# Attention stages with small heads: row maxima lead the weighing by one group and three key tiles instead of two whole groups

## The chip, the cores and the metric

The kernel runs on one core of a Trainium2 chip. The metric is the device time of one execution in microseconds (us): 5284.45 as the median of three runs, 5282.03 to 5288.88. Engines: TensorE (PE; its weight loads are PEld), VectorE (DVE), ScalarE (ACT), GpSimd (POOL) and SyncE (SP), which here only issues DMAs.

## The reference, cut to what matters

The program is a decoder of four layers, each with a self-attention, a cross-attention and a feed-forward part, each followed by a residual and a layer norm. Five of its attentions are softmax attentions over 16 heads of 16 channels, on a batch of 4 with 512 queries, and use the routine that is changed. Their core is

```
scores = einsum('bhqd,bhkd->bhqk', q, k) * scale   (+ bias or mask, or causal)
attn = softmax(scores, axis=-1)
out = einsum('bhqk,bhkd->bhqd', attn, v)
```

The routine runs six times. In the order of the program, with the name that its tiles have in the trace:

| stage | tiles' name | keys | key tiles of 128 |
|---|---|---|---|
| coarse levels of the pyramid attention | pyr_coarse | 512 places, each query sees 256 or 128 of them | 4 |
| fine level of the same | pyr_core | 512 | 4 |
| context (cross-attention of layer 1) | l1x_core | 1024 | 8 |
| plain (layer 2) | l2a_core | 512 | 4 |
| causal with a linear bias (layer 3) | l3a_core | 512, lower triangle | 4 |
| masked (cross-attention of layer 3) | l3x_core | 1024, with a mask that is added | 8 |

A seventh attention (heads of 64 channels) has a routine of its own and is not touched.

## The kernel before

`attention_stage` (L256) treats a batch b in four groups g of four heads, so 16 groups in a row. A group needs two things. The first is the maximum of each row of scores: `pass_a` (L546) multiplies queries by keys in chunks of up to 512 keys (TensorE, L558) into PSUM banks A, and `maxima` (L715) reduces each chunk on VectorE (L734; with a mask L730, which adds the mask tile `mask_q` first). A group has 16 chunks with four key tiles and 32 with eight. In the causal stage the four chunks that stand beside tile t span (t+1) x 128 keys, while the score products of tile t span (4-t) x 128 queries. The maxima then travel as a row: `turn` (L565) transposes them on TensorE (L572), `negate` copies them out on VectorE (L748, L751), `split_max` cuts them into three bf16 parts on GpSimd (L813, L814, L816), and `row` on SyncE writes them with three DMAs of 4 KB (L473) into three rows of the group's query tile. At the start of each group TensorE waits for these rows (`row_in`), because the score product then subtracts the maximum by itself.

The second is the weighing: for key tile i, four score products (L626, one a head) into banks B, four exponentials on ScalarE (L693), and in the next tile `weigh`, the product of weights and values (L593). In the masked stage each bank B is first filled with the mask tile `mask_k`, three fills of four by ScalarE (L676) and one by VectorE (L758), three steps ahead of the score product that adds to it. ScalarE and VectorE run their lists in order: a fill that waits for `mask_k` holds back every exponential and every maximum behind it.

While group g is weighed, the maxima of group g+2 are taken, a fair share beside each tile. So before group 0 can start, the maxima of groups 0 and 1 are taken alone, and beside the last two groups there are none. `turn` for group g+1 comes after tile 0 of group g.

SyncE's list for group g (L511 to L534) sets when transfers start. It runs strictly in order:
- wait until group g-1 is weighed (that is the end of tile 0 of group g), then load the values of group g+1 (L445) and queries and keys of group g+3 (L442);
- the row of group g+1 (waits for `split_max`);
- g = 0: `gather_sums` of the batch before, two DMAs of 32 KB, one after the other (L486, L488); VectorE's `invert_dense` waits for them after tile 0 of group 1;
- g = 1: `return_inverses`, one DMA of 32 KB and then four of 256 KB (L495, L498); GpSimd multiplies by them in groups 2 and 3 (L837), two products a group, after `split_max`;
- g = 3: `make_dense` of the batch before, eight DMAs of 64 KB (L507), after GpSimd's last product;
- masked stage, g = 1: the four tiles of `mask_q` of the next batch, each as soon as the maxima of group 3 have used the old one (L449);
- masked stage, g = 3: the four loads of `mask_k` of the next batch, 512 KB for two key tiles each (L452).

The fine stage also finishes the last batch of the coarse stage, so there these steps occur once more.

Of the kernel before, what the change touches and what calls it, by code (L numbers as in the profile page):

```python
# [255 lines left out]
def attention_stage(k, name, q_store, k_store, values, nq, nk, scale, att, head_dim=HD, slopes=None, mask=None, spans=None, dense_att=None, carried=None,  # L256
# [42 lines left out]
    inverse_at = [(2 + p, 0) for p in range(4)]  # L299

    def chunks_of(i):

        some = list(range(i * NCH // nkt, (i + 1) * NCH // nkt))
        return [some[len(some) * j // heads:len(some) * (j + 1) // heads] for j in range(heads)]
# [9 lines left out]
    with ExitStack() as held:  # L314
# [66 lines left out]
        def later(b, g, ahead):  # L381

            return b + (g + ahead) // groups, (g + ahead) % groups

        def keys_of(qi, c):
# [51 lines left out]
        def _(sync):  # L437
# [73 lines left out]
            def group(b, g):  # L511
                before = later(b, g, -1)
                if exists(*before):
                    sync.wait_ge(pv_done, at(*before, nkt, nkt + ahead_tiles))
                    if exists(*later(b, g, 1)):
                        load_values(*later(b, g, 1))
                    if exists(*later(b, g, RING - 1)):
                        load_group(*later(b, g, RING - 1))
                if exists(*later(b, g, 1)):
                    row(*later(b, g, 1))  # L520
                if g == 0 and to_finish(b - 1):
                    gather_sums(b - 1)
                if g == 1 and to_finish(b - 1):
                    return_inverses(b - 1)
                if g == 3 and to_finish(b - 1):
                    make_dense(b - 1)
                if mask is not None and g == groups - 3 and exists(b + 1, 0):
                    for qi in range(nqt):
                        sync.wait_ge(a_taken, at(b, groups - 1, NCH + 1, (qi + 1) * NCH // nqt))
                        load_mask_q(b + 1, qi)  # L530
                if mask is not None and g == groups - 1 and exists(b + 1, 0):
                    for i in range(nkt // 2):
                        sync.wait_ge(exp_done, at(b, g, NS, 2 * (i + 1) * heads + 3))
                        load_mask_k(b + 1, i)  # L534
# [10 lines left out]
        def _(pe):  # L545
# [60 lines left out]
            turn(0, 0)  # L606
            pass_a(0, 1, range(NCH))

            def group(b, g):
# [3 lines left out]
                for i in range(nkt):  # L613
                    more = chunks_of(i) if exists(*later(b, g, 2)) else [()] * heads
                    qs, ks = queries_of(i), slice(i * P, (i + 1) * P)
                    for j in range(heads):
# [16 lines left out]
                        mm.then_inc(s_ready, 1)  # L633
                        pass_a(*later(b, g, 2), more[j])
                    if i:
                        weigh(b, g, i - 1)
                    elif exists(*later(b, g, -1)):
                        weigh(*later(b, g, -1), nkt - 1)
                    if i == 0 and exists(*later(b, g, 1)):
                        turn(*later(b, g, 1))  # L640
# [65 lines left out]
        def _(dve):  # L706
# [71 lines left out]
            negate(0, 0)  # L778
            maxima(0, 1, range(NCH))

            def group(b, g):
                before = later(b, g, -1)
                for i in range(nkt):
                    more = chunks_of(i) if exists(*later(b, g, 2)) else [()] * heads
                    for j in range(heads):
                        after = step_after(b, g, i * heads + j)
                        if after[2] in by_vector and exists(*after[:2]):
                            fill(*after, at(b, g, NS, i * heads + j + 3))
                        maxima(*later(b, g, 2), more[j])
                        if (i, j) in inverse_at and not small and exists(*before):  # L790
                            invert(*before, inverse_at.index((i, j)))
                    if i == 0 and exists(*later(b, g, 1)):
                        negate(*later(b, g, 1))
# [2053 lines left out]
```

## Time and profile before

| | us |
|---|---|
| median of the runs (three) | 5284.45 |
| the profiled execution, its own time | 5285.31 |
| its span, first to last instruction | 5283.5 |
| mean granted TensorE clock, share of full speed | 0.882 |

The profile is of one execution. "Busy" is the time in which an engine ran something; a line of a group of instructions names the source line, the engine, and output and input tiles. PEclk is the share of the full 2.4 GHz that TensorE was granted; 0.50 is 1.2 GHz. The stage of each row can be told by its tiles' name or its time: coarse 156 to 324, fine 338 to 547, context 1482 to 1899, plain 2250 to 2458, causal 4309 to 4484, masked 4638 to 5173 us.

### The profile page before, as it was taken

What the parts mean: (1) busy time and instruction counts of PE and PEld (TensorE: products, weight loads), DVE (VectorE), ACT (ScalarE), POOL (GpSimd) and SP (SyncE); (2) the same over time, 40 slices, a digit from 0 to 9 for tenths busy, and PEclk for the clock granted to TensorE, in tenths of its full rate; (3) what the DMA queues carried; (4) which work ended last, traced back from release to release, by engine and by line L of the source; (5) the groups of instructions that cost most, each with busy time, mean ns of one, the idle gap of its engine ahead of it and who ended that gap; (6) DMA issues with size and microseconds to landing.
All of it is one profiled execution on the core that took longest, in us unless ns stands there. A gap on an engine that the chain in (4) does not pass through costs nothing. (4 is left out here: it accounts for less than half of the span.)

```text
span 5283.5 us, 69474 instructions
## 1 busy us (share of the span) xinstructions
PE 4269.9 (81%) x20468; PEld 2003.2 (38%) x20468; DVE 2857.8 (54%) x6454; ACT 2371.7 (45%) x4625; POOL 1389.1 (26%) x1234
## 2 busy tenths in 40 slices
PE   7779665666789968497699799999997979669986
PEld 5323454664422238223344233333335634312223
DVE  4458374015678830386300367666763256578875
ACT  4447231232346744265333344444441236349993
POOL 3111151221300020312000177777772112200001
PEclk9679877787779979788799899999998989769998
DMA  8655202430543336544233311112111065733421
GB/s 297 145 107 121 62 1 57 154 119 13 199 120 79 91 126 231 163 98 110 98 153 153 116 64 57 57 57 68 59 41 43 1 186 121 250 103 106 105 66 37
DMA packets 461222, 559.20 MB, mean 106 GB/s; under 512 B 80804, under 2 KB 363924, under 8 KB 448452
## 3 DMA queue, kind: packets, MB, share of 16 engines
q1 hardware_dynamic: 453440, 520.11, 33.0%
q0 software_dynamic: 6384, 32.61, 1.9%
q8 instruction: 138, 2.26, 0.2%
q10 hardware_dynamic: 1068, 2.66, 0.2%
q14 instruction: 192, 1.57, 0.1%
HBM read 340.80 MB, written 200.54 MB: 102 GB/s over the span
## 5 line engine op out<-in xcount | busy, mean ns | idle before, releaser
L1190 POOL TENSOR_TENSOR lc_totals<-lc_totals,lc_weights 128x1024 f32<-128x1024 f32 (+1 forms) x320 | 615.6, 1924 | 187.5 <-DVE lc_totals L1139 158.8
L1099 ACT ACTIVATE lc_weights<-ps 128x1024 f32<-128x1024 f32 x384 | 393.1, 1024 | 560.7 <-PE ps L1019 560.5
L1120 DVE TENSOR_REDUCE lc_part_max<-ps 128x2 f32<-128x1024 f32 x384 | 466.4, 1215 | 316.0 <-PE ps L999 316.0
L1019 PE MATMUL ps<-lc_q,lc_k 64*128 64x512 f32 x1536 | 394.2, 591 | 0.0
L1029 PE MATMUL ps<-lc_weights,lc_v 128*64 128x512 f32 x1536 | 373.3, 606 | 0.9 <-ACT lc_sums L1086 0.7
L734 DVE TENSOR_REDUCE l1x_core_part_max<-ps 128x1 f32<-128x512 f32 x512 | 317.0, 683 | 84.5 <-PE ps L558 78.3
L730 DVE CUSTOM_DVE_ANT_0 l3x_core_unused<-ps,l3x_core_mask_q 128x512 f32<-128x512 f32 x512 | 330.6, 686 | 7.0 <-DVE l3x_core_row_max L738 4.9
L693 ACT ACTIVATE l3x_core_weights<-ps 128x512 f32<-128x512 f32 x512 | 326.1, 691 | 7.7 <-PE ps L626 7.4
L189 ACT ACTIVATE proj_value<-ps 128x512 f32<-128x512 f32 (+2 forms) x352 | 179.9, 519 | 320.2 <-PE ps L159 267.6
L693 ACT ACTIVATE l1x_core_weights<-ps 128x512 f32<-128x512 f32 x512 | 266.3, 603 | 89.0 <-PE ps L626 88.9
L676 ACT ACTIVATE ps<-l3x_core_mask_k 128x512 f32<-128x512 f32 x384 | 269.3, 701 | 28.9 <-DMA l3x_core_mask_k<-in_mask_k 28.9
L558 PE MATMUL ps<-l3x_core_k,l3x_core_q 96*128 96x512 bf16 x512 | 214.4, 420 | 52.7 <-DVE l3x_core_part_max L730 37.6
L1185 POOL TENSOR_TENSOR lc_totals<-lc_weights 128x1024 f32<-128x1024 f32 x32 | 75.4, 2356 | 615.9 <-ACT lc_weights L1099 604.8
L558 PE MATMUL ps<-l1x_core_k,l1x_core_q 96*128 96x512 bf16 x512 | 210.5, 414 | 23.1 <-DMA l1x_core_k<-k_parts 16.3
L218 POOL TENSOR_TENSOR proj_parts<-proj_rest,proj_parts 128x512 bf16<-128x512 f32 x112 | 136.8, 1224 | 338.5 <-ACT proj_parts L169 338.1
L1111 DVE MEMSET lc_ones_row<- 128x128 bf16 x1 | 0.2, 165 | 397.3 <-PEq L112 397.3
L626 PE MATMUL ps<-l3x_core_q,l3x_core_k 99*128 99x512 bf16 x512 | 198.1, 393 | 19.1 <-ACT ps L676 18.1
L1295 PE MATMUL ps<-ident,X 128*128 128x128 f32 x352 | 69.8, 340 | 163.4 <-DVE X L1332 156.4
L999 PE MATMUL ps<-lc_k_round,lc_q_round 64*128 64x512 bf16 x768 | 151.4, 390 | 59.8 <-DVE lc_part_max L1120 48.6
L626 PE MATMUL ps<-l1x_core_q,l1x_core_k 99*128 99x512 bf16 x512 | 193.0, 387 | 6.4 <-ACT l1x_core_weights L693 6.4
L1316 DVE SCALAR_TENSOR_TENSOR rn_z<-ps,rn_z 128x256 f32<-128x256 f32 x112 | 45.9, 418 | 261.6 <-PE ps L1287 235.4
L734 DVE TENSOR_REDUCE l2a_core_row_max<-ps 128x1 f32<-128x512 f32 x256 | 158.5, 681 | 47.2 <-PE ps L558 47.1
(467 smaller groups left out, 8787.7 us busy)
## 6 DMA issues: line engine op xcount, KB each, us to landing
cf_w<-in_L1f_w SPq DMA_DIRECT2D x32, 1024.0 KB, 7.8
values<-proj_value SPq DMA_DIRECT2D x112, 256.0 KB, 3.2
latent_k<-proj_value SPq DMA_DIRECT2D x96, 256.0 KB, 2.0
latent_values<-proj_value SPq DMA_DIRECT2D x96, 256.0 KB, 2.0
lc_k<-latent_k SPq DMA_DIRECT2D x32, 768.0 KB, 6.5
lc_v<-latent_values SPq DMA_DIRECT2D x32, 768.0 KB, 5.1
k_parts<-proj_parts SPq DMA_DIRECT2D x56, 384.0 KB, 2.6
q_parts<-proj_parts SPq DMA_DIRECT2D x40, 384.0 KB, 3.1
```

The costliest lines, as they stand in the source:

```text
L189: nc.scalar.activation(value[0:rows, j % VALUES, :, 0:d], k.ps[0:rows, n % 8, 0:H * d].rearrange("p (h d) -> p h d", h=H), ACT.Copy).then_ ...
L558: mm = nc.tensor.matmul(out, q_stack[r][0:rows_a, j, qs], k_stack[r][0:rows_a, j, keys], start=True, stop=not causal)
L626: mm = nc.tensor.matmul(out, k_stack[r][0:rows_b, j, ks], q_stack[r][0:rows_b, j, qs], start=not seeded, stop=not (causal or seeded), skip ...
L676: nc.scalar.activation(k.ps[:, B0 + (g * NS + s) % B_BANKS, 0:nq], seed, ACT.Copy).then_inc(filled, 1)
L693: nc.scalar.activation(weights[:, (g * NS + s) % WEIGHTS, qs], k.ps[:, B0 + (g * NS + s) % B_BANKS, qs], ACT.Exp, scale=scale).then_inc(ex ...
L730: nc.vector.tensor_tensor_reduce(unused[:, n % 2, :], scores, mask_q[:, qi, keys], 1.0, -3.0e38, ALU.add, ALU.max, out).then_inc(a_taken, 1)
L734: nc.vector.reduce_max(out, scores, AX).then_inc(a_taken, 1)
L1019: mm = nc.tensor.matmul(out[j], k_tile[g % RING][strip(j), i * P:(i + 1) * P], q_tile[g % RING][strip(j), :], start=False, stop=True)
L1029: mm = nc.tensor.matmul(k.ps[strip(j), ACC, 0:nq], v_tile[g % V_RING][:, i, strip(j)], weights[:, i % TILES, j, :], start=i == 0, stop=i = ...
L1099: nc.scalar.activation(weights[:, i % TILES, :, :], k.ps[:, B0 + (i % 2) * HEADS:B0 + (i % 2 + 1) * HEADS, 0:nq], ACT.Exp, scale=scale).th ...
L1120: nc.vector.reduce_max(own, k.ps[:, A0:A0 + HEADS, :], AX).then_inc(a_taken, 1)
L1190: nc.gpsimd.tensor_tensor(total, total, own, ALU.add).then_inc(added_by_pool, 1)
```

## The change

The maxima now lead by one group and three key tiles. Beside tile i of group g stand the chunks of tile i+3, of group g+1 as long as i+3 is within the group, of group g+2 after that. Before group 0, only the chunks of three tiles of group 1 are taken ahead (12 of 16, or 12 of 32). `turn` and `negate` for group g+1 move from tile 0 to tile 1 (four key tiles) or tile 5 (eight). The loads of `mask_q` move from group 1 to group 2 and ahead of the row. Everything else that follows the row in SyncE's list keeps its place behind it.

```diff
--- before.py
+++ after.py
@@ -297,6 +297,8 @@
     QUARTER = nq // 4
     SUMS = 2
     inverse_at = [(2 + p, 0) for p in range(4)]
+
+    FIRST_TILES = min(nkt - 1, 3)
 
     def chunks_of(i):
 
@@ -382,6 +384,15 @@
 
             return b + (g + ahead) // groups, (g + ahead) % groups
 
+        def chunks_beside(b, g, i):
+
+            tile = i + FIRST_TILES
+            found = later(b, g, 1 + tile // nkt)
+            return (*found, chunks_of(tile % nkt) if exists(*found) else [()] * heads)
+
+        first_chunks = range(FIRST_TILES * NCH // nkt)
+        turn_at = nkt - FIRST_TILES
+
         def keys_of(qi, c):
 
             if spans:
@@ -516,6 +527,10 @@
                         load_values(*later(b, g, 1))
                     if exists(*later(b, g, RING - 1)):
                         load_group(*later(b, g, RING - 1))
+                if mask is not None and g == groups - 2 and exists(b + 1, 0):
+                    for qi in range(nqt):
+                        sync.wait_ge(a_taken, at(b, groups - 1, NCH + 1, (qi + 1) * NCH // nqt))
+                        load_mask_q(b + 1, qi)
                 if exists(*later(b, g, 1)):
                     row(*later(b, g, 1))
                 if g == 0 and to_finish(b - 1):
@@ -524,10 +539,6 @@
                     return_inverses(b - 1)
                 if g == 3 and to_finish(b - 1):
                     make_dense(b - 1)
-                if mask is not None and g == groups - 3 and exists(b + 1, 0):
-                    for qi in range(nqt):
-                        sync.wait_ge(a_taken, at(b, groups - 1, NCH + 1, (qi + 1) * NCH // nqt))
-                        load_mask_q(b + 1, qi)
                 if mask is not None and g == groups - 1 and exists(b + 1, 0):
                     for i in range(nkt // 2):
                         sync.wait_ge(exp_done, at(b, g, NS, 2 * (i + 1) * heads + 3))
@@ -604,14 +615,14 @@
                     nc.tensor.matmul(k.ps[:, B0 + n, 0:nq], *operands, start=True, stop=False, skip_group_check=True).then_inc(opened, 1)
             pass_a(0, 0, range(NCH))
             turn(0, 0)
-            pass_a(0, 1, range(NCH))
+            pass_a(0, 1, first_chunks)
 
             def group(b, g):
                 r = g % RING
                 if small:
                     pe.wait_ge(row_in, 48 * at(b, g, 1, 1))
                 for i in range(nkt):
-                    more = chunks_of(i) if exists(*later(b, g, 2)) else [()] * heads
+                    beside_b, beside_g, more = chunks_beside(b, g, i)
                     qs, ks = queries_of(i), slice(i * P, (i + 1) * P)
                     for j in range(heads):
                         s = i * heads + j
@@ -631,12 +642,12 @@
                         if causal:
                             mm = nc.tensor.matmul(out[:, 0:P], k.ident_bf[:, :], k.above_k[:, :], start=False, stop=True)
                         mm.then_inc(s_ready, 1)
-                        pass_a(*later(b, g, 2), more[j])
+                        pass_a(beside_b, beside_g, more[j])
                     if i:
                         weigh(b, g, i - 1)
                     elif exists(*later(b, g, -1)):
                         weigh(*later(b, g, -1), nkt - 1)
-                    if i == 0 and exists(*later(b, g, 1)):
+                    if i == turn_at and exists(*later(b, g, 1)):
                         turn(*later(b, g, 1))
                     if i == spread_at and not small and exists(*later(b, g, -1)):
                         spread(*later(b, g, -1), at(b, g, 1, 2 if exists(*later(b, g, 1)) else 1))
@@ -776,20 +787,20 @@
                         fill(0, 0, s, 1)
             maxima(0, 0, range(NCH))
             negate(0, 0)
-            maxima(0, 1, range(NCH))
+            maxima(0, 1, first_chunks)
 
             def group(b, g):
                 before = later(b, g, -1)
                 for i in range(nkt):
-                    more = chunks_of(i) if exists(*later(b, g, 2)) else [()] * heads
+                    beside_b, beside_g, more = chunks_beside(b, g, i)
                     for j in range(heads):
                         after = step_after(b, g, i * heads + j)
                         if after[2] in by_vector and exists(*after[:2]):
                             fill(*after, at(b, g, NS, i * heads + j + 3))
-                        maxima(*later(b, g, 2), more[j])
+                        maxima(beside_b, beside_g, more[j])
                         if (i, j) in inverse_at and not small and exists(*before):
                             invert(*before, inverse_at.index((i, j)))
-                    if i == 0 and exists(*later(b, g, 1)):
+                    if i == turn_at and exists(*later(b, g, 1)):
                         negate(*later(b, g, 1))
                     if i == 0 and g == 1 and to_finish(b - 1):
                         invert_dense(b - 1)
```

## Rows read from the trace of the kernel before

**Rows 1.** The page's first part: busy us, share of the span, instructions.
```profile
PE 4269.9 (81%) x20468; PEld 2003.2 (38%) x20468; DVE 2857.8 (54%) x6454; ACT 2371.7 (45%) x4625; POOL 1389.1 (26%) x1234
```
**Rows 2.** Busy time by stretch: start:end, length, engines, PEclk, DMA share, GB/s; context stage.
```profile
1503.00:1520.90 17.90, 17.82 (x31) 3.14 (x30) 17.90 (x31) 0.00 (x0) 1.21 (x3) 0.50 0.00 1
```
**Rows 3.** The same view, masked stage: second pass of maxima, then groups 0 to 13.
```profile
4677.60:4701.30 23.70, 18.38 (x32) 3.24 (x31) 20.99 (x92) 0.00 (x0) 1.22 (x3) 0.50 0.00 1
4701.30:5113.90 412.60, 382.52 (x1800) 99.82 (x1798) 367.24 (x1502) 401.21 (x797) 26.96 (x50) 0.98 0.36 94
```
**Rows 4.** Timeline (start, duration, engine, line), context stage, two tiles without maxima.
```profile
1864.50 1.07 PE L593 MATMUL ps<-l1x_core_weights,l1x_core_v 128*32 128x512 f32 x8
1866.95 0.64 PE L593 MATMUL ps<-l1x_core_weights,l1x_core_v 128*32 128x512 f32 x4
```
**Rows 5.** Timeline, coarse stage before group 0: one chain of the row, queues empty.
```profile
161.46 0.38 PE L572 MATMUL ps<-ident,pyr_coarse_row_max 128*16 128x128 f32 x1 [0.44 <-DVEq L740]
163.76 1.86 SPq L473 DMA_DIRECT2D pyr_coarse_q<-pyr_coarse_max_parts  x3
166.85 0.39 PE L626 MATMUL ps<-pyr_coarse_q,pyr_coarse_k 99*128 99x256 bf16 x1 [0.37 <-DMA pyr_coarse_q<-pyr_coarse_max_parts]
```
**Rows 6.** Timeline of TensorE, fine stage: one group, from first score to first score.
```profile
396.28 0.39 PE L626 MATMUL ps<-pyr_core_q,pyr_core_k 99*128 99x512 bf16 x1
...
399.30 0.28 PE L572 MATMUL ps<-ident,pyr_core_row_max 128*16 128x128 f32 x1
...
407.95 0.39 PE L626 MATMUL ps<-pyr_core_q,pyr_core_k 99*128 99x512 bf16 x1
```
**Rows 7.** SyncE's queue in that group; DMA issues (count, KB, median us to landing).
```profile
399.43 0.39 SPq L445 DMA_DIRECT2D pyr_core_v<-values  x1
...
pyr_core_q<-pyr_core_max_parts SPq DMA_DIRECT2D x42, 4.0 KB, 3.7
```
**Rows 8.** Timeline of TensorE, causal stage: starts of tiles 0, 2, 3, next group.
```profile
4363.47 0.39 PE L626 MATMUL ps<-l3a_core_q,l3a_core_k 102*128 102x512 bf16 x1
...
4368.96 0.28 PE L626 MATMUL ps<-l3a_core_q,l3a_core_k 102*128 102x256 bf16 x1
...
4371.42 0.23 PE L626 MATMUL ps<-l3a_core_q,l3a_core_k 102*128 102x128 bf16 x1
...
4373.73 0.39 PE L626 MATMUL ps<-l3a_core_q,l3a_core_k 102*128 102x512 bf16 x1
```
**Rows 9.** Coarse stage: TensorE's tiles 0 and 1; and who TensorE waited for.
```profile
201.96 0.39 PE L626 MATMUL ps<-pyr_coarse_q,pyr_coarse_k 99*128 99x256 bf16 x1 [1.05 <-DMA pyr_coarse_q<-pyr_coarse_max_parts]
...
204.36 0.38 PE L572 MATMUL ps<-ident,pyr_coarse_row_max 128*16 128x128 f32 x1
...
207.40 0.29 PE L626 MATMUL ps<-pyr_coarse_q,pyr_coarse_k 99*128 99x128 bf16 x1
...
PE ps L626 <- DMA pyr_coarse_q<-pyr_coarse_max_parts: 33.5, 14, 5.5
```
**Rows 10.** Masked stage: SyncE's queue in group 3 of batch 1; landing of a key mask.
```profile
4914.45 1.77 SPq L473 DMA_DIRECT2D l3x_core_q<-l3x_core_max_parts  x3
4917.01 6.32 SPq L507 DMA_DIRECT2D xT<-l3x_att  x8
4923.52 13.85 SPq L452 DMA_DIRECT2D l3x_core_mask_k<-in_mask_k  x4
...
l3x_core_mask_k<-in_mask_k SPq DMA_DIRECT2D x12, 512.0 KB, 3.7
```
**Rows 11.** Masked stage: ScalarE's same fill in two tiles; next group's first score.
```profile
4903.05 0.74 ACT L676 ACTIVATE ps<-l3x_core_mask_k 128x512 f32<-128x512 f32 x1
...
4906.51 0.78 ACT L676 ACTIVATE ps<-l3x_core_mask_k 128x512 f32<-128x512 f32 x1
...
4907.95 0.39 PE L626 MATMUL ps<-l3x_core_q,l3x_core_k 99*128 99x512 bf16 x1
```
**Rows 12.** DMA issues of the causal stage (count, KB each, median us to landing).
```profile
l3a_core_inverse<-inverse_sums SPq DMA_DIRECT2D x12, 256.0 KB, 4.4
```
**Rows 13.** Masked stage, timeline of TensorE after an idle stretch.
```profile
4880.01 0.61 PE L558 MATMUL ps<-l3x_core_k,l3x_core_q 96*128 96x512 bf16 x1 [3.43 <-DVE l3x_core_part_max L730]
```

## The prediction

> **What bounds the kernel now.** The page's shares come first: TensorE is busy 81% of the span, VectorE 54%, ScalarE 45% [rows 1]. They are averages over some forty stages, and the change touches six, so what counts is read inside those six: busy time by stretch, then the timelines of one group on TensorE and on SyncE, then the list of who waited for whom. The reader is to see four things.
>
> First, before group 0 nothing is weighed: the second pass of maxima of the context stage fills 17.9 us with VectorE at 17.9 and ScalarE at none, at a granted clock of 0.50 [rows 2]; in the masked stage 23.7 us [rows 3]. Second, inside the stages the pace is set by TensorE (fine, plain, context, causal) or ScalarE (masked, 401 of 412.6 us [rows 3]). One fine group takes 407.95 - 396.28 = 11.67 us, the turn starts 3.02 after its first score, so each later tile takes (11.67 - 3.02)/3 = 2.88, nearer 2.85 without the turn's own time [rows 6]; a tile without maxima beside it takes 1866.95 - 1864.50 = 2.45 [rows 4]. Third, the row's way from turn to the next group's first score is 166.85 - 161.46 = 5.4 us with empty queues, 2.3 of it before the first of three DMAs is issued and 1.9 for issuing them [rows 5]. Now it starts after tile 0, behind the loads issued at the same moment (a row DMA lands 3.7 us after issue there [rows 7], against 5.4 - 2.3 - 1.2 = 1.9 in rows 5), and is still hidden in four-tile groups, narrowly. Fourth, only the coarse stage waits for it now: 33.5 us in 14 waits [rows 9].
>
> **The change, part by part.** I call T the first score of a group, and count everything against the profiled execution.
>
> *The shorter start (a gain).* Group 1's last chunks leave the path before group 0. Context: 20 of 32 chunks at 17.9/30 = 0.60 us, 12.0 us (the row landed long before). Masked: 20 at 23.7/32 = 0.74, 14.8. Fine and plain: 4 chunks, 2.4 each. Coarse: nothing, since group 0 waits for its own row there [rows 5]; causal: its row also lands only about half a us before the end of the maxima, 0.6. Sum -32.2.
>
> *The same chunks beside the last-but-one group (a loss).* One tile (fine, plain, causal, coarse) or five (context) go from 2.45 to 2.85: 0.4 each in fine and plain and 2.1 in context. Masked: ScalarE sets the pace there, 0. In these groups the last row has only two tiles of 2.45 to hide 5.4: 0.4 more in each of fine, plain and context. Sum +4.1.
>
> *The later turn in fine, plain and context.* T to turn becomes 3.02 + 2.85 = 5.87, and 5.87 + 5.4 = 11.27 against a period of 11.67: hidden with 0.4 to spare. In context two tiles of 2.85 follow too. The loads ahead of the row had a whole tile more to drain. I take 0; if the cover is gone by half a us, 40 groups pay 20 us.
>
> *Causal.* The pattern of widths changes. Now tiles 0 and 1 take 4368.96 - 4363.47 = 5.5, tiles 2 and 3 4.8 [rows 8]. After the change the widest chunks (512) stand beside the widest scores (512): four chunks 384 columns wider, at 0.16 us each, add 0.6 to tile 0, while tile 1 loses 0.2 and tiles 2 and 3 lose 0.2 each. Turn at 5.5 + 0.6 - 0.2 = 5.9 by this, or 5.3 if the faster groups of the stage are the measure; I take 5.6; plus 5.4 is 11.0, while the tiles themselves end at 5.6 + 4.8 - 0.4 = 10.0. So the row ends last, in every group: 11.0 against 10.2 (this group 10.26 [rows 8]). Over some 13 groups 0.8 is 10; bounds 3 and 16.
>
> *Causal and coarse, groups with other traffic.* `make_dense` takes 6.3 us of SyncE, and started 0.8 after the row [rows 10]. The row's last issue moves from the start of the group to 1.2 us before T. So the loads of the next group 0 are issued at about T + 6 rather than T + 2.7, and the row of group 1 queues behind them until about T + 12.7: 1.8 too late, twice, in causal; 0.9 three times in fine and twice in plain; about 1 twice in coarse. `return_inverses` brings 1 MB (4.4 us each to landing [rows 12]) into the same queues as group 2's loads, 1.5 us later than now: 0.4 to 1 each in the four-tile stages, ten times. Sum: causal 5.6, fine 3.9, plain 2.6, coarse 3. With the 10 above and -0.6 at the start, causal is +15.
>
> *Coarse.* Here T to turn was 2.4 and tile 1 3.0 at half clock [rows 9]; at full clock, an estimate from half of these and ScalarE's part, 1.4 and 1.7. The turn moves to 4.9 or 3.1, plus 5.4 is 10.3 or 8.5, mixed 9.6; the rest of the tiles is shorter. Now a group takes (324 - 167)/16 = 9.8 on the mean, 2.4 of it waiting (33.5/14 [rows 9]), since the row queued behind loads, and by the new turn the loads have nearly drained. So the ordinary groups give 0 (bounds -15 if the clock stays up, +10); with the traffic and the first and last groups, which now have no loads ahead, +4.
>
> *Masked (the largest loss).* In SyncE's list of group 3 the loads of `mask_k` stand behind the row and `make_dense`. Same fill to same fill is 3.46 us a tile [rows 11]. The turn comes now 2.3 us before the row's first issue, at 4914.45 - 2.3 - 4907.95 = T + 4.2 [rows 10, 11], and after the change at T + 4.2 + 5 x 3.46 = T + 21.5; the row's last issue ends 2.3 + 1.8 later, T + 25.6. The next batch's first fill on ScalarE starts 1.4 us before its group [rows 11], at T + 4.2 + 7 x 3.46 - 1.4 = T + 27.0. After batch 0 no `make_dense` exists: load issued T + 25.7, landing 3.7 later [rows 10], T + 29.4, 2.4 late. After batches 1 and 2, from the row's issue start to the mask's is 4923.52 - 4914.45 = 9.1 us [rows 10], so T + 23.8 + 9.1 = T + 32.9, landing at T + 36.7, 9.7 late. ScalarE's two last exponentials and VectorE's last maxima stand behind these fills, so nothing hides it: 21.8 us. After such idle time TensorE runs at half clock for some matmuls (0.61 us instead of 0.39 for 512 columns, after 3.4 us of idle [rows 13]): 1.5 us each time, 4.5. The moved loads of `mask_q` have two tiles and more; 1 us for the first tile's load, which now queues behind group 2's other traffic. The row itself lands at T + 27, hidden. Masked: -14.8 + 21.8 + 4.5 + 1 = +12.5, taken as +12. Bounds for the stalls: 12 (make_dense wholly overlapped) to 30.
>
> The Trainium skill ("DMA: Bandwidth & Descriptors", section "Anatomy of one DMA — SWDGE (gpsimd) path") puts a DMA at about 2.0 us plus its bytes over 436 GB/s; as an estimate that page gives 3.2 us for a mask load and takes 1.5 us off the sum of the three stalls. The row has 3.7, and is used.
>
> *VectorE's `invert_dense`.* `gather_sums` now starts at about T - 1.5 and its two chained DMAs need some 3.8 us, to T + 2.3, before VectorE reaches the wait at about T + 3: 0.
>
> Sum by stage: coarse +4; fine -2.4 + 0.8 + 3.9 = +2; context -12.0 + 2.1 + 0.4 = -9.5; plain -2.4 + 0.8 + 2.6 = +1; causal +15; masked +12. Together +25: 5285.3 becomes 5310 in its profile. The median of the runs lies 0.9 below the profiled execution, so 5309.
>
> **The rivals.**
>
> *A. The row chain is exposed everywhere, or the causal stage loses its clock.* For: only 0.4 us of slack, and coarse, the one stage that idles before each group, runs at a mixed clock [rows 9]. Against: the context and fine chains have no loads ahead any more. Price: 0.5 x 40 groups = 20, or in causal half clock in its first tiles, 5.6 us becoming 8 or so, +2.4 x 10 = 24. About 5330. That idleness throttles the array to 1.2 GHz and activity releases it is the rule of the Trainium skill ("TensorE: Matmul & The Clock Gate", section "What's actually happening"); by that rule this rival gains, and rows 13 agrees with it.
>
> *B. No difference.* Rows no longer land behind loads, so coarse goes to its chain at full clock, 8.5 in place of 9.8 over 12 groups (-15), and causal keeps its pace (-10). For: the 33.5 us of waits there are mostly queueing. 5285.
>
> *C. Faster: the start's gain stands and the masked stage pays nothing.* Place: SyncE's list in group 3. If the key mask lands by T + 27.0, as it would if the old mask's release rather than the row were what SyncE waits for last, the three stalls (26 with the clock) vanish, and with B's causal term 5309 - 26 - 10 = 5273. It decides where the stalls sum to less than 14.8. Against: rows 10 shows SyncE strictly in order, with 9.1 us between.
>
> **How the numbers follow.** Forecast 0.52, A 0.18, B 0.15, C 0.1, the rest between or beyond. 0.2% (10.6 us) is about what a measurement of this kernel tells from no change. The forecast's own range is 5294 to 5326; to hold 8 in 10 with half of A and most of B, 5283 to 5332. Slower by over 0.2% (above 5295): nearly all of the forecast and A, 0.70. Within: 0.18. Faster: 0.12.
>
> **What would show it.** Start: context's first score 12 us earlier after its first maxima, masked 15. Masked: three new waits of ScalarE for `mask_k` from DMA, about 2, 10 and 10 us, and the loads (L452's place) right behind the row or `make_dense`. Causal: TensorE waits for the row before nearly every group, about 1 us, period 11.0. Fine, plain, context: no such waits outside groups 1 and 3 of a batch. Wrong if the mask waits are absent, if the 5.4 us chain lengthens or shortens by half a us, or if coarse changes by over 10 us.

## The result, and the profile after

The changed kernel takes 5340.2 us (median of four runs, 5338.57 to 5341.89) against 5283.24 (four) for the kernel before: ratio 1.0106, 95% interval 1.0094 to 1.0119. That is slower, as forecast, but by 57 us where 25 were forecast; the predicted range ended at 5332. The profiled execution has a span of 5336.8 us, 53.3 more than before, and the mean granted clock is 0.878, before 0.882.

The page's first line shows nothing of it: every engine is busy for the same time within 4 us as in [rows 1]. What grew is idle time.

```profile
PE 4270.7 (80%) x20468; PEld 2005.2 (38%) x20468; DVE 2860.5 (54%) x6454; ACT 2370.9 (44%) x4625; POOL 1387.6 (26%) x1234
```

So the reading goes by stage. The table gives each stage's length, from the first product of its maxima to the end of its last product of weights and values, from the two traces.

| us | before | after | difference | predicted |
|---|---|---|---|---|
| coarse | 167.7 | 183.2 | +15.5 | +4 |
| fine | 209.0 | 209.8 | +0.8 | +2 |
| context | 416.8 | 400.5 | -16.3 | -9.5 |
| plain | 208.3 | 209.6 | +1.3 | +1 |
| causal | 175.4 | 211.5 | +36.1 | +15 |
| masked | 535.0 | 553.7 | +18.7 | +12 |
| sum | | | +56.1 | +25 |

The stages' sum is 2.8 us more than the difference of the spans, so the rest of the program took that much less. How much a stage moves by itself is seen in the traces in which it has the old order, the one of the kernel before and those of the experiments below: coarse 164.6 to 167.7, context 414.2 to 419.9, causal 175.3 to 177.7, masked 534.2 to 536.2. A difference smaller than these ranges says nothing by itself.

Busy time by stretch, columns as in [rows 2]: after, the groups of the coarse, fine, causal and masked stage. The kernel before had a clock of 0.72, 0.98, 1.00 and 0.97 there. The reader is to see the PEclk column: 0.64 in coarse, 0.91 in causal.

```profile
168.10:340.80 172.70, 129.95 (x1011) 61.33 (x1011) 79.46 (x261) 79.42 (x271) 33.00 (x57) 0.64 0.46 106
370.00:562.80 192.80, 185.66 (x1012) 55.23 (x1010) 150.96 (x265) 140.15 (x271) 37.95 (x61) 0.98 0.47 104
4320.70:4519.20 198.50, 165.80 (x1495) 83.74 (x1495) 108.92 (x261) 111.46 (x272) 33.03 (x57) 0.91 0.40 94
4719.20:5225.20 506.00, 432.20 (x2020) 108.41 (x2018) 393.13 (x1584) 458.46 (x910) 33.14 (x57) 0.95 0.30 79
```

*Masked: the wait that was predicted.* Waits of the stage after (who waited for whom: total, times, longest), then SyncE's queue in group 3 of batch 1, and ScalarE's first fill and TensorE's first score of the batch after it. These answer to [rows 10, 11].

```profile
DVE ps L769 <- DMA l3x_core_mask_k<-in_mask_k: 23.6, 3, 10.1
ACT ps L687 <- DMA l3x_core_mask_k<-in_mask_k: 22.8, 3, 9.8
```

```profile
4960.71 1.77 SPq L484 DMA_DIRECT2D l3x_core_q<-l3x_core_max_parts  x3
4963.28 6.32 SPq L518 DMA_DIRECT2D xT<-l3x_att  x8
4969.80 6.10 SPq L463 DMA_DIRECT2D l3x_core_mask_k<-in_mask_k  x4
...
4973.90 0.60 ACT L687 ACTIVATE ps<-l3x_core_mask_k 128x512 f32<-128x512 f32 x1 [9.84 <-DMA l3x_core_mask_k<-in_mask_k]
...
4974.56 0.61 PE L637 MATMUL ps<-l3x_core_q,l3x_core_k 99*128 99x512 bf16 x1 [9.22 <-ACT ps L687]
```

The group's first score is at 4936.38. The row is issued at T + 24.3 (predicted 23.8), the mask's first load at T + 33.4 (32.9), the fill runs at T + 37.5 (36.7), and the next product has 0.61 us, half clock.

*Causal: the row ends last, and where it lands late the clock goes.* TensorE's turns and first scores of groups 6 to 10; the bracket is the idle time before and who ended it. In [rows 8] the groups followed each other in 10.26 us.

```profile
4400.31 0.28 PE L583 MATMUL ps<-ident,l3a_core_row_max 128*16 128x128 f32 x1
...
4407.22 0.39 PE L637 MATMUL ps<-l3a_core_q,l3a_core_k 102*128 102x512 bf16 x1 [2.37 <-DMA l3a_core_q<-l3a_core_max_parts]
...
4412.81 0.28 PE L583 MATMUL ps<-ident,l3a_core_row_max 128*16 128x128 f32 x1
...
4418.11 0.39 PE L637 MATMUL ps<-l3a_core_q,l3a_core_k 102*128 102x512 bf16 x1 [0.82 <-DMA l3a_core_q<-l3a_core_max_parts]
...
4431.61 0.60 PE L637 MATMUL ps<-l3a_core_q,l3a_core_k 102*128 102x512 bf16 x1 [3.43 <-DMA l3a_core_q<-l3a_core_max_parts]
...
4439.27 0.28 PE L583 MATMUL ps<-ident,l3a_core_row_max 128*16 128x128 f32 x1
...
4444.65 0.39 PE L637 MATMUL ps<-l3a_core_q,l3a_core_k 102*128 102x512 bf16 x1 [0.90 <-DMA l3a_core_q<-l3a_core_max_parts]
```

The group at 4407.22 is the one that was predicted: 4412.81 - 4407.22 = 5.6 to the turn, 5.3 for the row, period 10.9, and then 0.82 us of waiting. But the row before it took 6.9, and the row after it 7.9 (TensorE waits 3.43 us for it). The group behind that wait, at 4431.61, begins at half clock (0.60 for 512 columns) and turns after 7.7. In seven of the 15 groups the turn comes 6.7 to 7.7 us after the first score. The stretches from first score to turn at 4407.22 and at 4431.61, columns as in [rows 2], with the clock at 1.00 and 0.66:

```profile
4407.22:4412.81 5.59, 5.30 (x48) 2.56 (x49) 3.65 (x8) 4.49 (x9) 0.00 (x0) 1.00 0.20 62
4431.61:4439.27 7.66, 7.66 (x49) 3.32 (x50) 4.14 (x9) 4.52 (x9) 0.00 (x0) 0.66 0.16 47
```

It is the long waits that go with half clock, not the ordinary ones. Group by group, first the idle time before it, then the clock from its first score to its turn:

| idle before the group | groups | clock to the turn | score to turn |
|---|---|---|---|
| 0.7 to 1.7 us | 1, 2, 4, 6, 8, 10, 12 | 1.00 | 5.6 to 5.7 |
| 2.2 to 3.4 us | 3, 5, 9, 11, 13, 14 | 0.65 to 0.77 | 6.7 to 7.7 |
| 2.4 us | 7 | 1.00 | 5.6 |
| 1.1 us, clock at half since before the group | 0 | 0.76 | 7.2 |

Every wait of 2.2 us or more stands behind a row that took 6.7 us or more from turn to first score. SyncE's queue ahead of the row that was wanted at 4407 (four DMAs of inverses, 1 MB, then the loads of values and of queries and keys, then the row):

```profile
4395.26 1.70 SPq L509 DMA_DIRECT2D l3a_core_inverse<-inverse_sums  x4
4397.66 0.40 SPq L456 DMA_DIRECT2D l3a_core_v<-values  x1
4398.25 0.36 SPq L453 DMA_DIRECT2D l3a_core_q<-q_parts  x1
...
4402.69 1.78 SPq L484 DMA_DIRECT2D l3a_core_q<-l3a_core_max_parts  x3
```

The whole stage waits:

```profile
PE ps L637 <- DMA l3a_core_q<-l3a_core_max_parts: 28.8, 16, 3.4
```

*Coarse: the slow variant, or close to it, in every group.* TensorE's first score, turn and next first score of one group; in [rows 9] the turn came after 2.4.

```profile
209.64 0.28 PE L637 MATMUL ps<-pyr_coarse_q,pyr_coarse_k 99*128 99x256 bf16 x1 [2.09 <-DMA pyr_coarse_q<-pyr_coarse_max_parts]
...
211.09 0.39 PE L637 MATMUL ps<-pyr_coarse_q,pyr_coarse_k 99*128 99x256 bf16 x1
...
213.92 0.38 PE L583 MATMUL ps<-ident,pyr_coarse_row_max 128*16 128x128 f32 x1
...
219.41 0.28 PE L637 MATMUL ps<-pyr_coarse_q,pyr_coarse_k 99*128 99x256 bf16 x1 [2.05 <-DMA pyr_coarse_q<-pyr_coarse_max_parts]
```

TensorE begins at full clock (0.28 for 256 columns), falls to half after a tile (0.39), and turns after 4.3 us; with 5.5 for the row the group takes 9.8. Five others take 4.8 + 5.4 or 5.5, that is 10.2 to 10.3.

### The profile page after: what moved, and what is told of

Its sections match the earlier page's. It is cut to its first block and busy times, and to the rows that moved or that the text cites. A ratio compares the mean times of both kernels' runs of the same rounds, so it can differ in the third digit from the quotient of the medians.

```text
span 5336.8 us, 69480 instructions
## 1 busy us (share of the span) xinstructions
PE 4270.7 (80%) x20468; PEld 2005.2 (38%) x20468; DVE 2860.5 (54%) x6454; ACT 2370.9 (44%) x4625; POOL 1387.6 (26%) x1234
## 5 line engine op out<-in xcount | busy, mean ns | idle before, releaser
L637 PE MATMUL ps<-l3x_core_q,l3x_core_k 99*128 99x512 bf16 x512 | 200.7, 396 | 37.2 <-ACT ps L687 36.1
L745 DVE TENSOR_REDUCE pyr_core_row_max<-ps 128x1 f32<-128x512 f32 x256 | 158.4, 679 | 45.4 <-PE ps L569 45.3
```

The costliest lines, as they stand in the source:

```text
L637: mm = nc.tensor.matmul(out, k_stack[r][0:rows_b, j, ks], q_stack[r][0:rows_b, j, qs], start=not seeded, stop=not (causal or seeded), skip ...
L745: nc.vector.reduce_max(out, scores, AX).then_inc(a_taken, 1)
```

## The experiments

All have the kernel before as their base unless said otherwise, and each ratio is against runs of it on the same chip.

### Which stage pays

e1 has the new order in the causal stage alone, e2 in fine, context, plain and masked, e7 in coarse alone. A stage that keeps the old order gets a lead of all its tiles:

```diff
-    FIRST_TILES = min(nkt - 1, 3)
+    FIRST_TILES = nkt if name in (...) else min(nkt - 1, 3)
```

> The new order in the causal stage alone, all other stages as before. If the stages' losses are independent, the causal stage takes 36 us longer than before (175.4 to 211.5 us from its first maxima to its last weighing), and the whole program 36 us, 5319. Rival: the stages disturb each other (code fetches, transfers that cross stage borders), then it is under 25 or over 45.

> The new order in the fine, context, plain and masked stages, the coarse and causal stages as before. From the two traces: fine +0.8, context -16.3, plain +1.3, masked +18.7, so +4.5 us, 5288. Of context's -16.3 about 10 is the shorter start; 6 are stalls of all engines at the loop's start that the trace of before has in groups 6 and 10 and that of after has not. If these belong to the code's layout and not to the change, they may return here, and the sum is +10.

> New order in the coarse stage alone. The stage took 183.2 in the changed kernel against 167.7 before; if that is the stage's own doing it takes 183 here too: +15, 5296. Theory: T to turn 4.6 at half clock, chain 6.3 (not the 5.4 with empty queues), TensorE idle before each group, granted clock about 0.64. Rival: part of it is left over from other changed stages or from chance between executions (coarse differs by 2 us between executions of unchanged code): then under +8.

| | median us | ratio (interval) | stages with the new order |
|---|---|---|---|
| e1 | 5317.54 | 1.0065 (1.0048 to 1.0083) | causal 208.8, +33.5 |
| e2 | 5285.13 | 1.0009 (0.9999 to 1.0018) | fine 208.0, context 400.3, plain 208.7, masked 554.2 |
| e7 | 5296.95 | 1.0030 (1.0018 to 1.0041) | coarse 183.1, +15.5 |

The losses are the stages' own and add up: 0.65 + 0.09 + 0.30 = 1.04% against 1.06%. In e2 context's -16.5 cancels most of masked's +19.

### The causal stage: queue or clock

e3 issues the loads of queries and keys behind the row (the values' load stays ahead).

```diff
-                    load_group(*later(b, g, RING - 1))
...
                     row(*later(b, g, 1))
+                    load_group(*later(b, g, RING - 1))
```

> As the first of these runs (causal stage alone), but SyncE issues the row of group g+1 ahead of the loads of queries and keys of group g+3 (the load of values stays ahead). If the row's transfer waits behind these loads, the way from turn to landing is 5.1 to 5.4 us in every group instead of 6.2 on the mean, TensorE idles under 1.3 us before each group, keeps 2.4 GHz and the causal stage loses some 12 (queue) plus up to 12 (clock) us less than in the first run: +12 to +24. If the wide chunks beside the wide scores are the cause, it stays at +36.

5310.56, ratio 1.0057 (1.0040 to 1.0073); the causal stage stays at 208.7. The chain from turn to landing fell from 6.15 (e1) to 5.55, but a new wait stood in its place, TensorE's first product of maxima for the loads (the second line):

```profile
PE ps L639 <- DMA l3a_core_q<-l3a_core_max_parts: 18.4, 15, 2.4
PE ps L571 <- DMA l3a_core_k<-in_slopes: 11.2, 10, 1.8
```

With the shorter lead the first chunk of group g+2 is multiplied beside tile 1 of group g, so the loads can't be put off either: both transfers are wanted at once.

The run also shows what a short wait does to the clock. From 4379.65 to 4488.87 TensorE waits 0.8 to 1.5 us for the row before each of the eight groups that begin there, and the clock stays full:

```profile
4379.65:4488.87 109.22, 86.82 (x861) 45.61 (x859) 66.03 (x163) 61.26 (x151) 20.88 (x35) 1.00 0.46 113
```

The expectation had the clock kept and the stage shorter. Over this stretch the clock was kept, and its groups still took 12.5 us on the mean, since the turn came after 5.9 to 8.0 us at full clock. Earlier in the stage the clock did fall, in two groups behind waits of 1.9 and 2.2 us.

e4 leaves the order of e1 and keeps TensorE at work while it waits: six extra products, which nothing reads, before the wait for the row. e14 has three of them.

```diff
+                    pe.wait_ge(negated, at(b, g, 1, 1))
+                    for _ in range(6):
+                        nc.tensor.matmul(k.ps[:, SIDE, 384:512], k.ident[:, :], k.ident[:, :], start=True, stop=True)
                     pe.wait_ge(row_in, 48 * at(b, g, 1, 1))
```

> As the first of these runs (causal stage alone), and before each group, while TensorE would idle for the row, it multiplies the identity by itself six times (f32, 128 columns, some 1.5 us) into an unused part of a bank; nothing reads it. If half clock after these idle stretches is what makes a group's first two tiles 7.0 to 7.7 us in every second group instead of 5.6, they are 5.6 in nearly all groups and the stage is 10 to 14 us shorter than in the first run. If the clock is not the cause, it is the same or up to 8 us longer.

> New order in the causal stage alone with three extra products in place of six before the wait for the row (0.7 us, which fits into the 0.9 us that TensorE waits there). Theory (all of the prediction's terms for this stage hold at full clock, and what it left out is the clock): T to turn 5.6, ordinary period 10.9 to 11.0, stage 188 to 192 (+13 to +16 as predicted, against +33.5 without extra products), kernel +12 to +16, 5297. Rival (three don't keep the clock, or the row's traffic costs the rest): clock below 0.96, or a stage of 196 and more at full clock.

The groups of the causal stage in e1, e4 and e14 (PEclk third from the end):

```profile
4318.00:4514.00 196.00, 164.20 (x1495) 84.08 (x1495) 108.66 (x261) 111.86 (x272) 33.12 (x57) 0.92 0.40 95
```

```profile
4320.00:4505.00 185.00, 174.93 (x1671) 100.90 (x1675) 107.45 (x261) 111.09 (x272) 33.09 (x57) 0.99 0.42 100
```

```profile
4315.00:4503.00 188.00, 172.09 (x1585) 92.92 (x1585) 108.21 (x261) 111.42 (x273) 33.15 (x57) 0.96 0.42 98
```

| causal stage | length | clock | score to turn, mean | turn to landing, mean | ratio (interval) |
|---|---|---|---|---|---|
| e1 | 208.8 | 0.92 | 6.22 | 6.15 | 1.0065 (1.0048 to 1.0083) |
| e4, six | 198.2 | 0.99 | 5.68 | 5.75 | 1.0033 (1.0021 to 1.0046) |
| e14, three | 200.7 | 0.96 | 6.00 | 5.83 | 1.0034 (1.0022 to 1.0046) |

More work in TensorE's list made the stage 8 to 11 us shorter, so part of the loss is the clock. In e4 all groups but the first turn at full clock, after 5.6 us, and the ordinary period is 11.44, since the extra products themselves outlast the wait. In e14 it is 10.9 to 11.6 where the clock holds, but three groups still turned 1 to 4 us late: the first, and two behind waits of 2.7 and 2.1 us. My theory for e14, a stage of 188 to 192, did not come out; the rival's first branch (three products don't keep the clock) did.

### The coarse stage: the same test

e10 is e7 with the six products in the coarse stage, e12 the kernel before (old order everywhere) with them.

> New order in the coarse stage alone, and six extra products of 128 columns in float32 (into columns of bank SIDE that nothing reads, some 1.4 us at full clock, after the row's maxima have been copied out) before TensorE waits for the row. Theory (the stage turns at half clock in every group: 4.8 us from first score to turn, plus 5.3 for the row, is its period of 10.2; the clock is what costs): T to turn becomes 3.1 to 3.4, period 8.5 to 8.8 in ordinary groups, stage 183 - 15 x 1.6 = 159, kernel 5272 or so. Rival (the row's traffic and the late issue set the period, the clock only follows): stage stays above 178, kernel 5295.

> The kernel before, old order in every stage, with the same six extra products before the wait for the row in the coarse stage. Tells apart whether a gain of the coarse stage needs the later turn. Theory: the row queues behind the loads here (7.8 us from turn to landing); T to turn goes from 2.0 to 1.4 or so and the chain keeps its length, so the period falls from 9.96 to 9.3 at best, stage 158 to 164, kernel -4 to -9. If the clock plays no part under the old order: no change, 5284.

e10: 5297.98, ratio 1.0032 (1.0021 to 1.0042). The clock rose from 0.68 to 0.84, but the stage only fell from 183.1 to 178.7, and the time of the kernel didn't follow. Two ordinary groups that kept the clock took 8.7 and 8.9 us (3.4 + 5.3, 3.5 + 5.4); but in four groups the row lands 7.6 to 9.5 us after the turn, behind other transfers, and five others still turn after 4.6 to 6.1. The theory had 159 for the stage and 5272, the rival over 178 and 5295: the rival's numbers came out, though these two groups are near the theory's. So neither the clock alone nor the traffic alone sets this stage. e12: 5275.18, ratio 0.9990 (0.9981 to 1.0000), stage 161.8 against 164.6 to 167.7 in the traces with an unchanged coarse stage: kept busy, the old order gains 3 to 6 us in the stage, but in the kernel's time the gain is not clear of the noise (the interval reaches 1.0000).

### The place of the turn, and the masks

e5 has the new order in all stages, but turns one tile earlier, and issues the first two loads of `mask_k` ahead of the row. e8 has only context and masked in the new order, with the late turn and the early masks. e9 has only masked, with all four masks' loads behind the row but ahead of `make_dense`.

```diff
-        turn_at = nkt - FIRST_TILES
+        turn_at = nkt - FIRST_TILES - 1        # e5
...
+                if mask is not None and g == groups - 1 and exists(b + 1, 0):      # e5, e8: for i in range(2)
+                    for i in range(2):
+                        sync.wait_ge(exp_done, at(b, g, NS, 2 * (i + 1) * heads + 3))
+                        load_mask_k(b + 1, i)
                 if exists(*later(b, g, 1)):
                     row(*later(b, g, 1))
```

> New order in all six stages, with the turn one tile earlier (after tile 0, or tile 4 of eight) and the first two loads of mask_k ahead of the row. Theory (the late turn and SyncE's order make the loss; clock is a consequence): masked stage back to 535 - 14.8 = 520 with no wait for mask_k; the row starts 3 us earlier everywhere, so causal has T to turn near 3.5, its row queues behind loads again (7 us or so) and still lands before the tiles end: causal 178 (old 175), coarse 170 (old 168), fine and plain 206, context 400. Sum of stages about -30 against the kernel before, 5250. Rival (the narrow lead itself costs: VectorE's maxima of the last chunk are only just issued when the turn wants them): every turn waits for VectorE by 0.5 to 1 us, all six stages, 90 turns: +45 to +90 us on that, 5295 or more, with a wait of TensorE at the transpose (L583) for DVE in the lists.

> New order in context and masked only, the first two loads of mask_k ahead of the row. Theory: context -14 to -16.5 as in the two kernels measured so far, masked -14.8 and no waits for mask_k (520): together -29 to -31, 5251. Rival: the early loads of 512 KB lie in the way of the row or of the loads of the next group, so the masked stage keeps waits of 2 to 5 us at each of three batch ends and gains only 5: 5261. If context's -16 holds only by chance of the execution, it shows -9.5 and the whole is 5257.

> New order in the masked stage alone, with the loads of mask_k behind the row as in the changed kernel but ahead of make_dense. Theory (the stalls were 2.4 for the row's issue and 7.3 for make_dense): all three batch ends wait 2.4 us for mask_k, 7.2 together and up to 4.5 for the clock: masked stage 535 - 14.8 + 7 to 12 = 527 to 532, kernel -3 to -8, 5275. Rival (the transfers of 512 KB themselves or the release of the old mask set the landing, not SyncE's order): the waits stay near 10 us after batches 1 and 2, masked stage 545 or more.

| us | changed kernel | e5 | e8 | e9 |
|---|---|---|---|---|
| median | 5340.2 | 5293.56 | 5261.75 | 5285.92 |
| ratio (interval) | 1.0106 (1.0094 to 1.0119) | 1.0023 (1.0012 to 1.0034) | 0.9963 (0.9949 to 0.9977) | 1.0009 (0.9999 to 1.0018) |
| coarse | 183.2 | 165.4 | | |
| context | 400.5 | 415.4 | 400.8 | |
| causal | 211.5 | 187.9 | | |
| masked | 553.7 | 532.0 | 530.3 | 538.4 |

e5: one tile's difference in the turn is 18 us of coarse and 24 of causal. In coarse nothing is then left of the loss (165.4 against 164.6 to 167.7). Causal keeps 12.5. The turn waits for VectorE there in every group ("PE ps L587 <- DVEq L755: 9.6, 15, 0.8"), the wait that the rival named, but 4.2 of the 12.5 are the start and the first group, which waits 2.8 us for its row and then turns at half clock. In the masked stage the weight loads for the turn wait longer:

```profile
PEld ps L587 <- DVE l3x_core_row_max L753: 22.7, 12, 1.9
```

The theory had 5250 for e5, the rival 5295 or more; 5293.56 is close to the rival's number. But context alone accounts for 15 of the difference, and most of that is not this wait: the two groups at which a turn of the hardware loop begins take 30.5 and 29.3 us instead of 24.2 and 24.4.

e9: the three waits for the mask became alike and short (TensorE idles 2.3, 1.8 and 1.8 us; 2.4 was predicted for each), so the rest of the 9.7 was `make_dense`:

```profile
DVE ps L769 <- DMA l3x_core_mask_k<-in_mask_k: 8.5, 3, 3.2
ACT ps L687 <- DMA l3x_core_mask_k<-in_mask_k: 7.8, 3, 3.0
```

The stage is at 538.4 all the same, not 527 to 532. In e8 no wait for the mask is left, and it takes 530.3, not 520. So some 10 us of the start's gain are given back elsewhere (below). The kernel's 5261.75 is the number of e8's rival, but not for the rival's reason, which was waits that are not there.

### A version that beats both

> New order in coarse (with the six extra products), context, and masked (first two loads of mask_k ahead of the row); old order in fine, plain and causal. If the parts add up: -23 (as measured for context and masked) and -8 for coarse, 5254. If the coarse stage gains nothing from the kept clock, 5262 to 5275.

> New order in context and masked only, the first two loads of mask_k ahead of the row, old order elsewhere, and in the coarse stage the six extra products before the wait for the row. If the parts add up as measured one by one (-0.37% and -0.1%): ratio 0.995, about 5257. If they don't, 0.996 to 0.998.

e11 (e8 with e10's coarse stage): 5267.38, ratio 0.9978 (0.9969 to 0.9988); its coarse stage takes 182.7, so the new order costs there with the clock raised too (0.84). e13 is e8 with e12's coarse stage: 5254.25, ratio 0.9948 (0.9935 to 0.9962). The parts of e8 and e12 add up (0.37 + 0.10 = 0.47 against 0.52%), but the interval overlaps e8's (0.9949 to 0.9977), so what the extra products add to e8 is not clear of the noise. Coarse takes 162.6, context 399.6, causal in the old order 175.3, masked 528.3. It is 26 us faster than the kernel before, and by the two ratios 1.6% faster than the changed one.

## Why the prediction was right in direction and wrong in size

- **The row chain of 5.4 us, and fine and plain hidden by 0.4: right.** Ordinary fine groups turn at T + 5.87 and the row lands 5.2 later, period 11.67, as before [rows 6]. The row is late only in groups 4, 8 and 12, which take 12.6, 13.3 and 13.0: +3.8 in all, where +3.9 was predicted. The sum is right by some luck: 2.7 of it were to come from `make_dense`, in just these groups, and 1.2 from the inverses, which made no group of this stage late.
- **The shorter start: right.** Context -12.0 as predicted; masked -15.7 (predicted -14.8).
- **The wait for `mask_k`: right, mechanism and size.** TensorE idles 2.9, 9.2 and 8.9 us, 21.0 in all (predicted 21.8), and the groups after are 1.3 to 1.7 longer, 4.4 (predicted 4.5 for half clock). Rival C had the opposite and is out. The load of 3.2 us that follows as an estimate from the fit in the Trainium skill ("DMA: Bandwidth & Descriptors", section "Anatomy of one DMA — SWDGE (gpsimd) path") would have made this sum 1.5 us smaller. That fit is for DMAs that GpSimd issues, and these are issued by SyncE; the waits can't tell the two apart, since 21.0 lies 0.8 below the sum with 3.7 and 0.7 above the one with 3.2, but the load that held the group at 4974.56 went from issue to fill in 4.1.
- **Masked, "ScalarE sets the pace there, 0": mis-sized, +9.** 18.7 = -15.7 + 25.4 + 9.0. The first group takes 32.3 instead of 29.7: half clock lasts longer after the shorter start (in e8 0.50 for the first 8.7 us; before, 0.50 for 3.7 and then 0.77 for 5). Groups 6 and 10, where a turn of the hardware loop begins, take 35.6 and 35.4 instead of 33.5. The others take 29.0 instead of 28.7 to 28.85. e8, with no mask waits, has the same +10. ScalarE waits for a score product 18 times in the stage after, 11.0 us in all, where it did 6 times, 7.4 us. Whether the turn's new place does it stays open: in e5, which turns a tile earlier, the first group takes 32.7, the ordinary ones 29.4 and the two at the loop's turns 34.1, but there the turn also waits for VectorE.
- **Context: mis-sized in the other direction, -16.3 for -9.5.** The +2.1 for the last group is there (19.8 became 21.8). But the two groups at which a turn of the hardware loop begins took 30.1 and 25.5 us before and 24.2 and 24.4 after. That repeats: 27 to 30 in e7 and e9 (old order), 24.2 to 24.5 in the changed kernel and e8. In e5 it is 30.5 and 29.3, so it hangs on where the turn stands and not on the shorter lead; why, stays open.
- **Causal: the largest miss, +36 for +15.** The step that failed is "I take 5.6; plus 5.4 is 11.0" for every ordinary group, with 5.6 in all for other traffic: it has the whole stage at full clock, and the late rows too small. Where the clock is full the terms hold: 5.59 to the turn and, without traffic, a period of 10.9.

  Put together they give 12.9 for the start, 15 x (5.6 + 5.4), 5.6 of traffic and 8.6 for the last group, 192; that is +17, since I had counted 13 groups and left out the last row. The other 19 divide by place: the turn comes at 6.33 on the mean in place of 5.6 (15 x 0.73 = 10.9), from the turn to the next first score it is 6.27 in place of 5.4 and the traffic's share, 5.77 (15 x 0.50 = 7.5), and the last group is 0.9 longer, at a clock of 0.82.

  The 10.9 are rival A, which had a chance of 0.18, but not by the wait of about 1 us that the forecast put before every group. After waits of 0.7 to 1.7 us every group turned at full clock; the late turns (but the first) all follow waits of 2.2 to 3.4, and these stand behind rows that took 6.7 to 7.9. e1 has the same picture, the first group again aside: five of the eight groups behind waits of 2.1 to 3.4 us turned late, none of the six behind 0.7 to 1.2. So late rows cost twice, once as a wait and once as half clock behind it. That idleness slows the array and work keeps it up is also what the Trainium skill says ("TensorE: Matmul & The Clock Gate", section "What's actually happening"); e4 and e14 agree (clock 0.99 and 0.96 for 0.92).

  In e4 the turn costs 1.2 instead of 10.9; its other 4.9 above the 192 stand behind the turn, most of them extra products that outlast the row. In e14 8.6 are left: 6.0 in the turns (3.9 of it the first group's) and 2.6 behind them. Why the rows of this stage take 0.5 more on the mean than I had is known only in part: the loads and the inverses are issued just ahead of them (as in the queue shown above), and with the clock kept they take 0.3 to 0.4 less.
- **Coarse: "ordinary groups 0", +15.5 for +4.** My own half-clock branch (4.9 + 5.4 = 10.3) was near what happened in ordinary groups, 10.4 on the mean, and not the mean of two branches, 9.6. By groups: the eight ordinary ones went from 9.75 to 10.44 on the mean, +5.6; the first and the last two that wait for a row (0, 13 and 14), which had at most the load of the values ahead of it and so little to win, from 24.0 to 30.5 together, +6.5; the four with other traffic +3.0; the last group +0.5. Only the traffic and a part of the second were in my +4. e5 shows that all of it hangs on the turn's place. How much of it is the clock's is not settled: with the clock raised to 0.84 the stage took 178.7 in e10 and 182.7 in e11, for 183.1.

The forecast and rival A should not have been alternatives: the forecast had late rows in some causal groups, and [rows 13] showed half clock after 3.4 us of idle. Taking A's price for causal (24) and the half-clock branch for coarse ((10.3 - 9.8) x 12 = 6) would have given 5309 + 24 + 6 = 5339. That this is nearly the measured time is luck, since it is put together after the result, and by stages it would have been 3 us too high in causal, 7 too high in context, 6 too low in coarse and 7 too low in masked.

## What to carry to other kernels

If a change lets TensorE wait before groups of work, look at the longest of the waits and not at the ordinary one. Here 0.7 to 1.7 us of waiting left the next group's first tiles at full clock, while after 2.1 to 3.4 us they had half clock in 11 of 15 groups (the changed kernel and e1), and a chain that starts from that work (here the turn) got 1.1 to 2.1 us longer too. (In e3 and e5 it also fell after waits of 1.9 and 1.8.) In such groups count the wait and the half clock behind it. When a step in a software pipeline is moved later, walk down each queue that it is moved past in time: what stands behind it in order moves as well, whether it has to do with it or not (here a mask behind a row and eight copies). And shorten a lead only in those stages where the chain has room; the same edit gained 16 us in one stage and lost 36 in another.

## What was not expected of the hardware

Extra products made a kernel faster: six products without use before each causal group but the first raised the stage's clock from 0.92 to 0.99 and took it from 208.8 to 198.2 us (e1 to e4, ratio 1.0065 to 1.0033). And the start of a hardware loop's second and third turn costs between 1 and 7 us in the context stage, with the same instructions in another order (24.2 to 30.5 us for a group of 23.3 to 23.6); the start of its first turn, at group 2, costs nothing of the kind. Why is not known.
